# Bias tables without a stage: lines made in the first stage, shifted rows of them copied in memory beside the causal attention

## The reference

```python
bucket = _relative_position_bucket(mem - ctx)   # 32 buckets, constant beyond a distance
values = rel_emb[bucket]                        # one value for each of 16 heads
att = jnp.einsum('bhqd,bhkd->bhqk', q, k) * (1.0 / math.sqrt(HS))
att = att + compute_bias(rel_emb, t, t)
att = jax.nn.softmax(att, axis=-1)
```

## Time and profile before

| | us |
|---|---|
| median of 3 runs | 7709.58 (7699.38 to 7716.36) |
| profiled execution | 7715.76 |
| its span | 7714.1 |
| mean granted TensorE clock, share of full speed | 0.914 |

### The profile page before, as it was taken

The page is one execution under the profiler, slowest core; times in us unless marked ns, Lnnn a source line. Parts: engine busy times, 40 slices in busy tenths (PEclk is TensorE's granted clock), DMA queues, the critical chain, the costliest instruction groups (busy, mean ns, idle before and its releaser), DMA issues. The chain is left out here.

```text
span 7714.1 us, 120187 instructions
## 1 busy us (share of the span) xinstructions
PE 6384.6 (83%) x31364; PEld 3277.2 (42%) x31364; DVE 4755.7 (62%) x12029; ACT 2770.5 (36%) x6066; POOL 1252.2 (16%) x779
## 2 busy tenths in 40 slices
PE   6788858989987976899994387887996888998979
PEld 2333334655455533222222263334553455544555
DVE  4656557733763534899985747984335764347635
ACT  0255514712463210466661104541110354224611
POOL 1100016100620002000000003550002431015100
PEclk9899979989998988899997599998998999999999
DMA  5422245541455245333323211114222455324541
GB/s 176 115 64 65 54 132 155 181 141 59 147 169 185 75 176 199 103 81 76 87 55 108 90 70 53 37 39 132 66 63 83 132 163 175 93 88 147 170 149 55
DMA packets 931101, 850.48 MB, mean 110 GB/s; under 512 B 222216, under 2 KB 785377, under 8 KB 930465
## 3 DMA queue, kind: packets, MB, share of 16 engines
q1 hardware_dynamic: 500624, 522.99, 23.7%
q10 hardware_dynamic: 430080, 323.08, 13.1%
HBM read 503.10 MB, written 346.00 MB: 110 GB/s over the span
## 5 line engine op out<-in xcount | busy, mean ns | idle before, releaser
L1252 ACT ACTIVATE Catt_E<-Catt_t 128x512 f32<-128x512 f32 x1024 | 576.3, 595 | 341.2 <-DVE Catt_t L1215 259.9
L1189 DVE CUSTOM_DVE_ANT_0 Catt_S<-Catt_s,Catt_win 128x1024 f32<-128x1024 f32 x512 | 621.5, 1215 | 6.9 <-DMA Catt_win<-skewed 5.4
L1189 DVE CUSTOM_DVE_ANT_0 Aatt_S<-Aatt_s,Aatt_win 128x128 f32<-128x128 f32 (+7 forms) x512 | 375.4, 756 | 250.6 <-PE Aatt_s L1118 245.0
L1252 ACT ACTIVATE Aatt_E<-Aatt_t 128x512 f32<-128x512 f32 (+3 forms) x768 | 353.8, 489 | 283.5 <-PE Aatt_t L1150 177.4
L1147 PE MATMUL Catt_t<-Catt_Q,Catt_K 123*128 123x512 bf16 x1024 | 369.7, 388 | 58.2 <-ACT Catt_E L1252 28.3
L1118 PE MATMUL Catt_s<-Catt_K,Catt_Q 96*128 96x512 bf16 x1024 | 320.9, 396 | 25.4 <-DMA Catt_K<-k_parts 12.5
L1215 DVE TENSOR_TENSOR Catt_t<-Catt_t,Catt_near 128x256 f32<-128x256 f32 (+2 forms) x640 | 281.7, 457 | 75.1 <-PE Catt_t L1147 67.6
L1169 PE MATMUL Catt_o<-Catt_E,Catt_V 128*32 128x256 f32 x4096 | 327.9, 392 | 0.0
L1147 PE MATMUL Aatt_t<-Aatt_Q,Aatt_K 99*128 99x512 bf16 (+3 forms) x768 | 245.2, 337 | 63.4 <-ACT Aatt_E L1252 34.6
L2343 PE MATMUL scan_cum<-scan_X,scan_upto 128*128 128x512 f32 x512 | 265.6, 609 | 24.7 <-DVE scan_X L2412 23.3
L2341 PE MATMUL scan_cum<-scan_X,scan_after 128*128 128x512 f32 x448 | 240.6, 619 | 44.1 <-DVE scan_pi L2423 44.1
(11 more groups left out here) (721 smaller groups left out, 14466.6 us busy)
## 6 DMA issues: line engine op xcount, KB each, us to landing
moe_cb<-c_s SPq DMA_DIRECT2D x16, 1024.0 KB
bias_rows<-line SPq DMA_DIRECT2D x16, 960.0 KB, 6.5
skewed<-bias_win ACTq DMA_DIRECT2D x16, 960.0 KB
Catt_win<-skewed SPq DMA_DIRECT2D x16, 960.0 KB, 4.8
rec<-state_in_r ACTq DMA_DIRECT2D x32, 416.0 KB
scan_r<-rec SPq DMA_DIRECT2D x64, 208.0 KB, 2.5
Aatt_Q<-q_parts SPq DMA_DIRECT2D x32, 384.0 KB, 4.3
Aatt_K<-k_parts SPq DMA_DIRECT2D x32, 384.0 KB, 5.4
```

Source lines behind the costliest of these rows:

```text
L1189: v.tensor_tensor_reduce(out=S[:, j % 2, 0:w], in0=s_ps[j % 2][:, 0:w], in1=win[:, 0 if causal else h, w0:w0 + w], scale=-1.0, scalar=BIG, ...
L1252: a.activation(E[:, kb % NB, h, lo:hi], t_ps[n % 2][:, 0:hi - lo], ACT.Exp, scale=scale).then_inc(exped, 1)
```

## The change

The stage `bias` is gone. `stage_enter` gets a `BiasTables` object that makes the lines: SP loads the embedding and the one-hot matrix before the copies of x, TensorE and DVE compute the line before their other work, and SP waits for DVE, stores `lines`, waits for the store, and then issues `back`, a copy of 512 values of each line in reverse order, element by element, and the two `sides`. POOL and DVE make the `ext` table behind their other work in this stage, and SP stores it behind its last load of x.

In `Aatt` each `load` issues two more DMAs (`spread_lines`), from memory to memory: 2 heads x 32 shifted rows of `lines` into `skewed`, 2 x 32 shifted rows of `back` into `near_s`. Over 32 steps this fills both tables. The rows step backwards by one element. SP's stream is written out instead of looped, and SP waits for all copies at the end of the stage. `Catt` reads the tables as before.

```diff
+    def product(self, t):
+        t.wait_ge(self.loaded, 32)
+        for c in range(0, 2 * T, 512):
+            ins = t.matmul(self.ps[0:self.H, c:c + 512], self.emb[:], self.hot[:, c:c + 512], start=True, stop=True)
+        ins.then_inc(self.lined, 1)
+
+    def copy(self, v):
+        v.wait_ge(self.lined, 1)
+        v.tensor_scalar(self.out[:], self.ps[0:self.H, :], 4.0, None, ALU.mult).then_inc(self.copied, 1)
+
+    def store_lines(self, sp):
+        sp.wait_ge(self.copied, 1)
+        sp.dma_start(self.lines, self.out[:]).then_inc(self.stored, 16)
+        sp.wait_ge(self.stored, 16)
+        sp.dma_start(self.back.unsqueeze(2), bass.AP(self.lines.tensor, self.lines.offset + T + 2 * P - 1, [[2 * T, self.H], [-1, 4 * P], [1, 1]]),
+                     allow_slow_non_contiguous=True).then_inc(self.ext_out, 16)
+        for i, col in enumerate((0, 2 * T - 1)):
+            sp.dma_start(self.sides[:, i:i + 1], self.lines[0:self.H, col:col + 1].unsqueeze(0).to_broadcast([NT, self.H, 1]),
+                         allow_slow_non_contiguous=True).then_inc(self.sides_in, 16)
...
+    def store(self, sp):
+        sp.wait_ge(self.ext_done, 1)
+        for k in range(PARTS):
+            sp.dma_start(self.ext_s.rearrange("(h k u) c -> k u h c", k=PARTS, u=NT)[k],
+                         self.ext[:, k].rearrange("p u c -> p (u c)")).then_inc(self.ext_out, 16)
+        sp.wait_ge(self.ext_out, 16 + 16 * PARTS)
...
@@ stage_enter
             tables.load(sp, logs)
+            bias.load(sp)
             for b in range(B):
                 sp.dma_start(act0["rows"][b * TP + PAD:(b + 1) * TP, :], x[b * T:(b + 1) * T, :]).then_inc(copied, 16)
+            bias.store_lines(sp)
             sp.wait_ge(zeroed, 1)
...
+            bias.store(sp)
             sp.wait_ge(pads, 16 * 2 * B * len(acts))
...
@@ stage_thin_attention
+            def spread_lines(it, b):
+                lines, back, windows, nears = aside
+                up, down = lines[it * 2:it * 2 + 2, P - 1 - b * 32:2 * T], back[it * 2:it * 2 + 2, P - b * 32:4 * P]
+                for src, out, step, w in ((up, windows, 2 * T, 2 * T - P), (down, nears, 4 * P, 3 * P)):
+                    sp.dma_start(out.rearrange("(h p) c -> h p c", p=P)[it * 2:it * 2 + 2, b * 32:(b + 1) * 32, :],
+                                 bass.AP(src.tensor, src.offset, [[step, 2], [-1, 32], [1, w]])).then_inc(spread_out, 16)
...
-                if b == 0 and isinstance(it, int):
+                if b == 0 and isinstance(it, int) and it == 0:
                     sp.wait_ge(V_ones, 1)
...
+                if aside:
+                    spread_lines(it, b)
...
-            pipelined(sp, PAIRS, B, ((3, maxima), (0, load)))
+            if aside:
+                written_out(sp, PAIRS, B, ((3, maxima), (0, load)))
+                sp.wait_ge(spread_out, 32 * B * PAIRS)
+            else:
+                pipelined(sp, PAIRS, B, ((3, maxima), (0, load)))
...
-def stage_bias_tables(nc, rel_emb, onehot, line, skewed, near_s, ext_s):
...
-    stage_bias_tables(nc, i["L1_attn_rel_emb"], i["onehot"], line, skewed, near_s, ext_s)
```

More of the change, by code:

```diff
@@ L297, in stage_enter @@
+def stage_enter(nc, x, act0, acts, tables, logs, bias):
     with ExitStack() as ctx:
@@ L299, in stage_enter @@
         tables.working(pl)
+        bias.working(pl)
         xin = pl.sb("xin", [P, IN, C])
@@ L333, in _ @@
             make_identity(nc, g, ident, made)
+            bias.place(g)
         @block.tensor
@@ L337, in _ @@
             t.sem_inc(t_done, IN)
+            bias.product(t)
             t.wait_ge(made, 1)
@@ L370, in _ @@
         def _(v):
+            bias.copy(v)
             tables.make(v)
+            bias.split(v)
 def stage_project(nc, name, src, width, w, out, res, base=None, bias=None, norm=True, act=ACT.Copy,
@@ L925, in _, with stage_thin_attention @@
                 a.wait_ge(z_out[i], 16 + 16 * B)
-def stage_thin_attention(nc, name, q_s, k_s, v_s, nm_s, r_s, oT_s, scale, bias=None):
+def stage_thin_attention(nc, name, q_s, k_s, v_s, nm_s, r_s, oT_s, scale, bias=None, aside=None):
     causal = bias is None
@@ L1009, in stage_thin_attention @@
         o_out = [pl.sem(f"o_out{i}") for i in range(B)]
+        spread_out = pl.sem("spread_out")
         if not causal:
@@ L2956, in bass_post_layernorm_stack @@
     tables = RecurrenceTables(nc, kept)
-    stage_enter(nc, i["L0_attn_x"], a0, acts, tables, i["L3_logs"])
+    lines, back, skewed, near_s = scratch("lines", [16, 2 * T]), scratch("back", [16, 4 * P]), scratch("skewed", [16 * P, 2 * T - P]), scratch("near_s", [16 * P, 3 * P])
+    ext_s = nc.dram_tensor("ext_s", [16 * PARTS * NT, T], BF16, kind="Internal").ap()
+    stage_enter(nc, i["L0_attn_x"], a0, acts, tables, i["L3_logs"], BiasTables(i["L1_attn_rel_emb"], i["onehot"], lines, back, ext_s))
     cur = a0
@@ L2960, in bass_post_layernorm_stack @@
               (i["rope_cos"], i["rope_sin"]), q_parts, k_parts, v_s, 1.0)
-    stage_thin_attention(nc, "Aatt", q_parts, k_parts, v_s, nm_s, r_s, oT_s, 0.25)
+    stage_thin_attention(nc, "Aatt", q_parts, k_parts, v_s, nm_s, r_s, oT_s, 0.25,
+                         aside=(lines, back, skewed, near_s))
     stage_thin_out(nc, "Aout", oT_s, i["L0_attn_W_proj"], a1, a0, bias=i["L0_attn_b_proj"])
@@ L2964, in bass_post_layernorm_stack @@
     cur = local_transformer("B", "L0_ffn", cur)
-    line, skewed, near_s = scratch("line", [16, 2 * T]), scratch("skewed", [16 * P, 2 * T - P]), scratch("near_s", [16 * P, 3 * P])
-    ext_s = nc.dram_tensor("ext_s", [16 * PARTS * NT, T], BF16, kind="Internal").ap()
-    stage_bias_tables(nc, i["L1_attn_rel_emb"], i["onehot"], line, skewed, near_s, ext_s)
     nxt = a1 if cur is a0 else a0
```

161 lines of the change are left out of this document (42 added, 119 removed).

## The result

| | before | changed |
|---|---|---|
| median, us | 7704.48 (7697.91 to 7716.36, 4 runs) | 7842.76 (7832.15 to 7855.26, 4 runs) |
| ratio | 1 | 1.0177, 95% interval 1.0164 to 1.0190 |
| profiled span, us | 7714.1 | 7840.2 |

The changed kernel is 1.8% slower. The prediction was 7778 us, range 7690 to 7920, "slower" at 0.76. The sign and the range held. The time came out 65 us above the prediction, nearly half as much as the whole change.

The account below looks back on a forecast made before the run. TensorE was busy 83% of a span of stages separated by barriers, each judged by its own limit. Profiled 7715.8 - 133.6 (bias) + 190 (Aatt) + 12 (first stage) gave 7784, adjusted to the median as 7778 us; range 7690 to 7920.

Parts of the forecast that it names:

- Bias stage, -133.6: Bias stage between two barriers: removing it gains its whole length on the path, 133.6 us.
- Aatt, +190: Causal attention: two-engine copies delay the maxima's reload and the product by key; 162 us over 28 periods plus 28 at the start.
- predicted 162: Aatt: copies of steps 4 to 31 lengthen 28 periods by 5.8 us each.
- predicted 28: Start of Aatt: three copies queued with loads 0 to 2 put the first product by key 27.6 us later.
- L: Aatt: the issue of a step's Q load, from which times in a period of 20.93 us are counted.
- S: Aatt: time of one step's copies on two engines, taken as 13.5 us, from 11.4 to 18.4.
- 31 x S - 228: Aatt: general formula for the added us from S; 121 at 11.3, 342 at 18.4.
- R2: Rival in Aatt: two engines at 26 GB/s or more each, deciding point S = 11.3; 7650 to 7715 us, chance 0.08.
- The slack of 8 us: Aatt: copies cost nothing while S stays below a period's slack of about 8 us.
- R1: Rival in Aatt: copies hidden, on four or more engines or over 36 GB/s each; 7588 us, chance with R4 0.12.
- First stage, +12: First stage: x loads 7.7 us later, 2 for the reversed copy, 2 for the far table's stores; 8 to 55.
- Rival R3: Slower: other queue's small pieces delayed in Aatt, or reversed copy at its upper bound; 7850 to 8000 us, chance 0.08.

Follow-up runs that it names:

- the run with 16 heads: Changed kernel with each table copy in Aatt taking 4 rows of all 16 heads instead of 32 rows of 2: 7654.49 us, ratio 0.9927 to the kernel before.
- 16 rows (S = 7.0): Changed kernel with 16 of each copy's 32 rows in the Aatt loop, the others copied behind it with outermost dimension 16: 7684.14 us, Aatt 757.6.
- 24 rows (S = 9.9): Changed kernel with 24 of each copy's 32 rows in the Aatt loop, the others copied behind it with outermost dimension 16: 7708.52 us, Aatt 784.8.
- the run behind the maxima: Changed kernel with the 2-head copies issued on SP behind the maxima and ahead of the next load: 7845.73 us, Aatt 903.4.
- straight: Changed kernel with the element-by-element reversed copy replaced by an unreversed store of 16 rows from the chip: 7747.85 us, first stage 75.8.
- the run with 4 heads: Changed kernel with each table copy in Aatt taking 16 rows of 4 heads: 7673.57 us, Aatt 746.7.

## Why the prediction was right, and where it was not

- **Bias stage, -133.6.** Right: barriers stood at both ends.
- **Aatt, +190; measured 190.4.** The mechanism is the one named: the copies run on two engines (the run with 16 heads takes the loss away) and the product by key waits for the reload. The last 28 periods grew by 160.7 in all, predicted 162; the start lost 22.5, predicted 28 (the first product by key moved by 20.2, predicted 27.6); what follows the last load grew by 7.2, predicted nothing. That the sum came out to the microsecond is luck, since three sizes inside a period were off as well and made up for each other:
  - The copies. In the trace their packets run from L+5.4 to L+18.3 in the mean, so S is 12.9 (11.9 to 13.6 in single steps), and that already holds what the other queue takes; the forecast had 13.5 and 1.0 beside it. By my formula 31 x S - 228 this would be 172. 12.9 us is 22.9 GB/s for each engine, and it is above the 11.3 at which R2 decides. The 56 GB/s of the window hold the other queue's stores and are no mark of R2.
  - The reload. It is issued earlier than forecast, at L+18.8 instead of L+21.4, but in the period shown it takes 3.7 us to land, not 1.4 (649.05 to 652.76): Rb's packets ran from 648.8 to 652.1, and those of the reload only from 651.7 on. So the product starts at L+22.5, predicted 22.8.
  - The clock. From there to the next load it takes 4.95 us instead of 3.82, as the clock has fallen to its lower level in the idle time. The clock was in the sum at nothing: a sum of waits alone leaves out what TensorE pays after a wait.
- **The slack of 8 us.** Near: 16 rows (S = 7.0) lose nothing in an ordinary period, 24 rows (S = 9.9) lose 0.9. But the slack was worked out for the maxima alone, and the run behind the maxima lost as much through Rb. Its 5.0 us stood in the earlier trace rows; what they become when Rb is issued while the copies run, 12.2 us, was the question not asked. R1 took four engines to be hidden, and there the once-a-pair loss cost 29.3 us.
- **First stage, +12; measured +110.7.** The mis-sized term is the reversed copy, taken at 16 ns of an engine for each element, 8 us. It came to some 154 ns by the hold of SP's queue (78.86 us for 512 elements an engine) and 186 ns by the start of the x loads, above even the upper bound of 103. The rest was nearly right: without this copy the stage costs +12.5 (straight) or +14.0 (turned by VectorE), where 7.7 for the x loads and 2 for the stores had been set. Both bounds were prices of something else. The side loads write into the chip, where an element of the copy costs 31 ns; they bound nothing for a write into memory. The pads do move at some 12 ns of an engine when queued up, as shown above, but they come from the chip and are 16 B long. Nor does the recorded time of a packet give its price. The DMA queues of the changed kernel from 20 to 60 us and from 60 to 70 us (packets, MB, share of 16 engines):

```profile
q1 hardware_dynamic: 3129, 0.01, 5.0%
q1 hardware_dynamic: 2699, 0.01, 100.1%
```

Each packet has 4 B, so each element is indeed a transfer of its own. In the first stretch 5.0% of 16 x 40 us over 3129 packets is 10.2 ns each, like the pads; but they come 205 ns of an engine apart. In the second they come 59 ns apart and are recorded as taking all of it. The copy has no even pace, and no run shows what sets it. The row that could have warned is that SP can be held for long at one small DMA. In the kernel before, at a pad,

```profile
7.43 5.03 SPq L319 DMA_DIRECT2D rows<-enter_zero  x1
q1 hardware_dynamic: 64, 2.10, 129.5%
```

it is held for 5.03 us instead of 0.4. The second line is the queue in these 5 us: 2.10 MB in 64 packets, the copies of x and no piece of a pad. So there it was the large copies ahead that held SP. Rival R3 had this case at 53 us, with too small a bound and 0.08.
- **The other stages, 0; measured -41.** Not in the sum, and not to be had from the rows of before; 31 of it are B1att and H1att, moe another 8 (534.4 to 526.1), whose cause was not looked for.
- **The prediction's 65 us** are thus +99 in the first stage and -41 elsewhere; the 7 us left are the difference of medians and profiles.

## What to carry to other kernels

Look at the outermost dimension of both sides of a copy before its bytes: with 2 there, 18.9 MB cost 190 us, and with 16 there the same bytes cost nothing. A gap in the DMA queues is room only if every small transfer that uses the same engines, on both queues and in either order, has its slack too. Where a wait is forecast for TensorE, put its clock into the sum as well: in Aatt a third of the loss was longer products. Price a copy of single elements by a copy of the same kind (same size of piece, memory or chip at either end), and by the time that passes, not by the busy share of a stretch. Keep such copies from memory to memory out of a queue that anything waits for: VectorE, reading with a step of -1, made the same reversed lines in 0.67 us.

## What the runs showed of the hardware that I had not expected

- A 4-byte element copied backwards from memory to memory cost 134 to 154 ns of an engine by the hold of the queue, and 163 to 187 by the start of the x loads (113.39 in the run with 4 heads, 125.10 in the changed kernel, against 29.91); forwards 116 and 140; from memory into the chip 34 and 31. A piece of 16 B from the chip into memory cost some 12 ns.
- The hold falls on the DMA issued next, whatever it is: 77.76 us on a load of 128 elements, 34.22 us on a store of 16 rows.
- The granted clock fell to 0.50 in a wait of 5.4 us of TensorE and was still 0.50 after 7 us of work (656 to 660). The way from the first product to the next load took 1.1 us longer with it; over Aatt the same products took 62.6 us more.
- The same local attention takes 243 to 246 or 257 to 261 us, with none or two unexplained waits of VectorE; moving or removing a stage ahead of it in the program changed which.
- ACT lost 4.4 to 5.1 us once a pair, with no cause in the profile, in the kernels whose copies run on two or four engines ahead of the maxima; in those with 16 its longest such wait was 3.6 us, and none fell at that place of the pair.
